# A graph network's first norm by groups of blocks, early loads of x, node numbers in PSUM, and fewer early scatters

## The reference

```python
edge_index = jnp.stack([src, dst])
h = jnp.maximum(_layernorm(x, axis=-1), 0.0)
x = x + _L0_gnn_ref(h, edge_index, L0_gnn_weight, L0_gnn_bias)
h = jnp.maximum(_layernorm(x, axis=-1), 0.0)
x = x + _L1_gnn_ref(h, edge_index, L1_gnn_W, L1_gnn_att_src, L1_gnn_att_dst, L1_gnn_bias)
...
```

```python
def mobius_add(x, y, c):
    x2 = jnp.sum(x * x, axis=-1, keepdims=True)
    y2 = jnp.sum(y * y, axis=-1, keepdims=True)
    xy = jnp.sum(x * y, axis=-1, keepdims=True)
    num = (1.0 + 2.0 * c * xy + c * y2) * x + (1.0 - c * x2) * y
    den = 1.0 + 2.0 * c * xy + c * c * x2 * y2
    return num / jnp.maximum(den, MIN_NORM)
...
def mobius_matvec(m, x, c):
    sc = jnp.sqrt(c)
    xn = _safe_norm(x)
    mx = x @ m.T
    mxn = _safe_norm(mx)
    res = jnp.tanh(mxn / xn * _artanh(sc * xn)) * mx / (mxn * sc)
...
res = proj(mobius_matvec(weight, x, c), c)
hyp_bias = proj(expmap0(b, c), c)
res = proj(mobius_add(res, hyp_bias, c), c)
xt = logmap0(res, c)
support_t = jax.ops.segment_sum(xt[s], r, num_segments=N_NODES)
```

## Time and profile before

| | us |
|---|---|
| median of 3 runs | 8386.53 (8385.81 to 8389.94) |
| the profiled execution, its own time | 8386.38 |
| its span in the profile | 8384.7 |
| POOL busy | 5866.1 (70% of the span) |
| DVE busy | 3407.2 (41%) |
| PE busy | 3380.2 (40%) |
| ACT busy | 1148.5 (14%) |

### The profile page before, as it was taken

How to read it: one execution, slowest core, us unless ns; L and a number is a source line. 1 busy time by engine, 2 the same in 40 slices (tenths; PEclk the granted TensorE clock), 3 DMA queues, 4 the chain that set the end, 5 groups by cost and what they waited for, 6 DMA issues and landing times.

```text
span 8384.7 us, 80823 instructions
## 1 busy us (share of the span) xinstructions
PE 3380.2 (40%) x13790; PEld 2554.1 (30%) x13791; DVE 3407.2 (41%) x7346; ACT 1148.5 (14%) x1948; POOL 5866.1 (70%) x5837
## 2 busy tenths in 40 slices
PE   1344443100002665442555543333345544455553
PEld 1244332100002555111444431111134444344442
DVE  4434656300004556992323323333343333433335
ACT  1000001333331111772000000000010000100001
POOL 0577777777777751787777777777757777477774
PEclk7555555555555666565555555555555555555555
DMA  1112111355553332001222222222222121111111
GB/s 39 52 51 50 45 46 33 92 135 135 135 135 84 87 86 67 19 27 39 70 70 70 69 65 77 77 76 77 76 54 52 52 53 52 48 52 53 52 52 47
DMA packets 348608, 555.47 MB, mean 66 GB/s; under 512 B 121171, under 2 KB 200871, under 8 KB 348511
## 3 DMA queue, kind: packets, MB, share of 16 engines
q0 software_dynamic: 199680, 357.35, 17.7%
q1 hardware_dynamic: 148831, 197.20, 7.8%
HBM read 448.57 MB, written 105.56 MB: 66 GB/s over the span
## 4 chain that ended last, share of the span: by engine, by line
POOL 41%; issue 21%; PE 16%; DVE 10%; DMA 7%; DVEq 4%; ACT 1%; SPq 0%; ACTq 0%; POOLq 0%
POOL GATHERED L619 34%; PE PS L730 15%; POOL list_dram L632 7%; DVE OH L1315 2%; DMA GATHERED<-row_tab,SRCI 2%; DMA GATHERED<-typed_b_tab,PLACE 2%; DVEq L317 1%; DVE OH L1309 1%; DMA GATHERED<-gat_tab,SRCI 1%; DVE T L1120 1%; DVE SM L1130 1%; DMA gat_rows<-GATHERED 1%; DMA GATHERED<-typed_tab,KEYF 1%; DVEq L319 1%; DVE T L1705 1%
## 5 line engine op out<-in xcount | busy, mean ns | idle before, releaser
L730 PE MATMUL PS<-GATHERED,OH 128*128 128x128 f32 (+2 forms) x9216 | 2434.1, 441 | 3059.1 <-DVE OH L1309 688.3
L619 POOL DMA_INDIRECT GATHERED<-row_tab,SRCI x2496 | 2466.4, 988 | 1157.8 <-issue 688.1
L730 PEld LDWEIGHTS PS<-GATHERED,OH 128*128 128x128 f32 (+1 forms) x9216 | 1899.7, 300 | 3651.7 <-issue 2182.7
L632 POOL DMA_INDIRECT list_dram<-REC,PLACE x832 | 973.8, 1170 | 507.7 <-issue 261.5
L619 POOL DMA_INDIRECT GATHERED<-typed_b_tab,PLACE x832 | 816.0, 981 | 261.7 <-issue 224.8
L619 POOL DMA_INDIRECT GATHERED<-typed_tab,KEYF x832 | 818.1, 983 | 253.6 <-issue 241.1
L619 POOL DMA_INDIRECT GATHERED<-gat_tab,SRCI x832 | 785.0, 943 | 253.6 <-issue 222.8
L1315 DVE TENSOR_SCALAR OH<-IOTA,DSTF,WF 128x128 f32 x2048 | 581.5, 360 | 433.3 <-issue 406.9
L1332 DVE TENSOR_TENSOR T<-T,PS 128x128 f32 x512 | 146.8, 287 | 962.7 <-PE PS L730 961.2
L730 PE MATMUL PS<-T,OH 128*128 128x132 f32 x2048 | 426.6, 382 | 241.2 <-DVE OH L1309 141.1
L730 PEld LDWEIGHTS PS<-T,OH 128*128 128x128 f32 x2048 | 383.1, 280 | 284.7 <-issue 193.2
(11 more groups left out here) (268 smaller groups left out, 3415.0 us busy)
## 6 DMA issues: line engine op xcount, KB each, us to landing
gat_rows<-GATHERED SPq DMA_DIRECT2D x208, 264.0 KB, 2.3
GATHERED<-gat_rows SPq DMA_DIRECT2D x208, 264.0 KB
GATHERED<-row_tab,SRCI POOLq DMA_INDIRECT x2496, 2.5
ROWI<-dst_rows SPq DMA_DIRECT2D x208, 128.0 KB
typed_b_tab<-ACC SPq DMA_DIRECT2D x49, 384.0 KB, 2.4
list_dram<-REC,PLACE POOLq DMA_INDIRECT x832
GATHERED<-gat_tab,SRCI POOLq DMA_INDIRECT x832
GATHERED<-typed_tab,KEYF POOLq DMA_INDIRECT x832, 2.5
```

Source lines behind the costliest of these rows:

```text
L619: pool.indirect_dma_start(out=rows_at[:, u * CT + t, 0:width], out_offset=None, in_=table, in_offset=bass.IndirectOffsetOnAxis(ap=rows[:, ...
L632: pool.indirect_dma_start(out=list_dram, out_offset=bass.IndirectOffsetOnAxis(ap=PLACE[:, t:t + 1], axis=0), in_=REC[:, 2 * t:2 * t + 2], ...
L730: last = mm(bank(p)[:, 0:r.shape[1]], onehot(p, t, 1, onehots_), r, start=(t == 0), stop=(t == CT - 1))
```

## The change

1. **Loads.** The weight of layer 0 and its bias come first (s_first), then x in two parts, 21 and 28 blocks (s_x), then the edges (s_edges), then everything else (s_in).
2. **First norm and product by groups.** `norm_groups("l0")` waits for parts of x alone; `dense_groups("l0")` multiplies by W0X, 129 columns, whose last is W0 times the bias, so that the product of each row with the bias falls out as a column. ACT also squares the transposed rows (HTSQ), and PE sums them with a column of ones: the row norms (HN2). `product_rows` on ACT copies the product to T, its square to H, the bias column to SM; `squared`, five groups late, sums the squares on DVE. The norm of the Moebius sum is worked out from the sums (seven operations on 128x49) and no longer from the table. The bias step goes by groups: ACT makes scaled bias rows for 49 blocks, DVE multiplies and adds, and each group has a store of its own; POOL waits for all seven.
3. **Placement.** `edge_rows`, `chunk_ends`, `edge_columns` and `source_blocks` hold what DVE did with the edges, and stand between the parts of the above, while ACT answers. Copies of WT and WL2 go from DVE to ACT, the clear of ACC from DVE to POOL.
4. **Scatters.** EARLY is 64 instead of 96; MIDDLE stays 432, so 368 follow g1.
5. **PSUM.** COLUMN (the node numbers that one-hots compare with), SAME and PLACEF (two operands of the ranks) lie in PSUM banks 2 to 7, which no walk but gb uses. COLUMN is copied again after gb's part in PSUM is over, and before l2b.

```diff
-    EARLY = 6 * BATCH
-    MIDDLE = EARLY + 21 * BATCH
+    EARLY = 4 * BATCH
+    MIDDLE = EARLY + 23 * BATCH
...
-        SAME, BEFORE, PLACEF, BUCKET = (EX[:, k * NT:(k + 1) * NT] for k in range(4))
+        BLOCK_OF, BEFORE, BUCKET = (EX[:, k * NT:(k + 1) * NT] for k in range(3))
+        PLACEF, COLUMN, SAME = (PS[:, 1024 * k:1024 * k + NT] for k in (1, 2, 3))
...
+            load(W0N, w0, s_first)
+            bcast(YROW, b0.rearrange("a b -> (a b)"), s_first)
+            for k, b0_ in enumerate(X_PARTS):
+                a, b = b0_ * GB, (X_PARTS[k + 1] * GB if k + 1 < len(X_PARTS) else NB - 1)
+                load(X3[:, a:b, :], x[a * P:b * P, :].rearrange("(b p) f -> p b f", p=P), s_x[k])
+            load(X3[0:LASTN, NB - 1, :], x[(NB - 1) * P:N, :], s_x[1])
...
+            for g in range(NG):
+                sp.wait_ge(s_tab, g + 1)
+                sp.dma_start(row_tabs[0][g * GB * P:(g + 1) * GB * P, :].rearrange("(b p) f -> p b f", p=P),
+                             group(T3, g)).then_inc(s_stored, 16)
...
+            pool.wait_ge(s_pair, 1)
+            pool.wait_ge(s_wt, 3)
+            pool.memset(ACC[:, :], 0.0).then_inc(s_zero, 1)
...
-            pool.wait_ge(s_stored, 16)
+            pool.wait_ge(s_stored, 16 * NG)
             walk("l0", row_tabs[0], D, SRCI)
...
                     for t in range(GB):
                         last = mm(product(g, t, F), HT[:, t * P:(t + 1) * P], w, start=True, stop=True)
+                    if squares:
+                        pe.wait_ge(ht_squared, n + 1)
+                        for t in range(GB):
+                            last = mm(HN2[:, g * GB + t:g * GB + t + 1], HTSQ[:, t * P:(t + 1) * P], ONE[:, :],
+                                      start=True, stop=True)
...
+            def product_rows(g):
+
+                columns_out(g, D + 1, 0, D, T3, ACT.Copy)
+                columns_out(g, D + 1, 0, D, H3, ACT.Square)
+                return columns_out(g, D + 1, D, D + 1, small(20).rearrange("p (b o) -> p b o", o=1), ACT.Copy)
...
-            norm_relu()
...
+            norm_groups("l0", X3, arrivals=X_PARTS, squares=5)
+
+            post()
+            edge_rows()
+            answered()
+            dve.sem_inc(s_rows, 1)
+            post()
+            ts(small(2), small(2), MIN_NORM, None, ALU.max)
+            chunk_ends()
+            answered()
...
-            tt(T3, T3, spread(small(21)), ALU.mult)
-            tt(H3, over(YROW, NB), spread(small(22)), ALU.mult)
-            tt(T3, T3, H3, ALU.add)
-            ask()
-            total(small(5), H3)
-            ask()
+            tt(small(5), small(5), small(21), ALU.mult)
+            tt(small(9), dot, small(22), ALU.mult)
+            stt(small(5), small(9), 2.0, small(5), ALU.mult, ALU.add)
+            tt(small(5), small(5), small(21), ALU.mult)
+            tt(small(9), small(22), small(22), ALU.mult)
+            stt(small(5), small(9), y2, small(5), ALU.mult, ALU.add)
+            ts(small(5), small(5), 0.0, None, ALU.max)
...
+            for g in range(NG):
+                tt(group(T3, g), group(T3, g), spread(group_of(21, g)), ALU.mult)
+                dve.wait_ge(n_biased, g + 1)
+                tt(group(T3, g), group(T3, g), group(H3, g), ALU.add)
+                dve.sem_inc(s_tab, 1)
...
-                                           column[:, bass.ds(c * CT, CT)].rearrange("p (t o) -> p t o", o=1)
+                                           COLUMN[:, bass.ds(c * CT, CT)].rearrange("p (t o) -> p t o", o=1)
```

More of the change, by code:

```diff
@@ L299, in program @@
         typed_mm = sem("typed_mm")
-        denses = {"l0": 0}
-        norms = {n: k for k, n in enumerate(("l1", "l2", "l3a", "l3b", "out"))}
+        norms = {n: k for k, n in enumerate(("l0", "l1", "l2", "l3a", "l3b", "out"))}
         stores = {"l3a": 1, "l3b": 2}
@@ L901, in answer, with norm_groups @@
                 nc.scalar.activation(out_, in_, fn, **kw).then_inc(s_act, 1)
[L903 to L921 removed]
+            def norm_groups(name, out_rows=None, scaled=False, relu=False, squares=False):
                 k = norms[name]
@@ L964, in attention_rows @@
-                return last
+                columns_out(g, F, 0, XW, A3, ACT.Copy)
+                return columns_out(g, F, XW, F, AM[:, :].rearrange("p (b k) -> p b k", k=HEADS), ACT.Copy)
             def scaled_rows(g):
@@ L971, in scaled_rows @@
                 return last
-            for req in requests["before_l0"]:
+            for req in requests["bias"]:
                 answer(*req)
-            dense(dn, denses["l0"], 1)
-            for req in requests["l0"]:
+            norm_groups("l0", product_rows, squares=True)
+            for req in requests["norms"]:
                 answer(*req)
+            act.wait_ge(s_wt, 2)
+            nc.scalar.activation(WT, PS[:, 0:4 * NT4 * D], ACT.Copy)
+            nc.scalar.activation(BCOL, PS[:, 2560:2560 + 2 * NT4], ACT.Copy).then_inc(s_wc, 1)
+            for req in requests["sum"]:
+                answer(*req)
+            act.wait_ge(s_wt, 3)
+            nc.scalar.activation(WL2[:, 0:NT4 * D], PS[:, 0:NT4 * D], ACT.Copy)
+            nc.scalar.activation(WL2[:, (NT4 + 1) * D:], PS[:, NT4 * D:2 * NT4 * D], ACT.Copy)
+            nc.scalar.activation(WL2[:, NT4 * D:(NT4 + 1) * D], PS[:, 2048:2048 + D], ACT.Copy).then_inc(s_wc, 1)
+            for req in requests["log"]:
+                answer(*req)
+            act.wait_ge(s_h, 2)
+            for g in range(NG):
+                for b in range(g * GB, (g + 1) * GB):
+                    last = nc.scalar.activation(H3[:, b, :], YROW, ACT.Copy, scale=small(22)[:, b:b + 1])
+                last.then_inc(n_biased, 1)
             wk = walks["l0"]
@@ new lines, in source_blocks @@
+            def source_blocks():
+                step(v.tensor_copy(SRCI[:, :], SRCF[:, :]))
+                dve.sem_inc(walks["l0"].free, RING)
+                step(v.tensor_copy(BLOCK_OF.bitcast(I32), SRCF[:, :]))
+                step(v.tensor_single_scalar(BEFORE.bitcast(I32), BLOCK_OF.bitcast(I32), 7, ALU.logical_shift_right))
+                step(v.tensor_copy(BUCKET, BEFORE.bitcast(I32)))
+                dve.wait_ge(s_drow, 64)
+                chunk_table(RANGEF, RANGES)
+                dve.sem_inc(s_info, 1)
@@ L1266, in normed, with squared @@
                     dve.sem_inc(n_normed, 1)
-                for s in range(NG + 2):
-                    for part, g in ((center, s), (variance, s - 1), (normed, s - 2)):
-                        if 0 <= g < NG:
-                            part(g)
+                def squared(g):
+                    dve.wait_ge(n_out, k * NG + g + 1)
+                    total(small(squares)[:, g * GB:(g + 1) * GB], group(H3, g))
+                parts = [(center, 0), (variance, 1), (normed, 2)] + ([(squared, 5)] if squares else [])
+                for s in range(NG + parts[-1][1]):
+                    for part, late in parts:
+                        if 0 <= s - late < NG:
+                            part(s - late)
             def artanh(o, n):
@@ L1289, in artanh, with onehots @@
                 tt(o, small(10), ser, ALU.add)
[L1291 to L1306 removed]
+            def onehots(c, b, p, weights=None, of=OH):
                 if weights is None:
@@ L1322, in all_added, with aggregate @@
                 hold(dve, wk.more_added, before + more + 1)
-            def aggregate(name, result, F, weights=None, ahead=None, column=DSTF, table=RANGES,
+            def aggregate(name, result, F, weights=None, ahead=None, table=RANGES,
                           parts=((NIT - 1, None, None),), sets=2, joins=False):
@@ L1380, in aggregate @@
                     read(0, 0, table)
[L1381 removed]
+                onehots(0, block_values(0)[2], 0, weights, of).then_inc(wk.onehot, 1)
                 start = 0
```

425 lines of the change are left out of this document (182 added, 243 removed).

## The result

The changed kernel takes 8134.89 us (median of 4 runs, 8128.51 to 8146.72), the kernel before 8388.24 us in the same series: a ratio of 0.9699, 95% interval 0.9685 to 0.9713. The forecast was 8074 us with a range of 8045 to 8130. The direction came as forecast, and so did the freeing of POOL's gathers. The size did not: the median lies 5 us above the range and 61 above the forecast, because waits between engines were left out or taken too short. The profiled execution took 8131.74 us with a span of 8130.0, 254.7 us less than before.

What follows compares the result with a forecast made beforehand. POOL and the issue time between its instructions were taken as the bound. Savings of 133 (first gather), 91 (l0 walk), 32 (scatters), 29 (l2) and 27 us (l2b) sum to 312, giving 8074 us, range 8045 to 8130.

Steps and rivals of the forecast that it cites:

- (b): What lengthens POOL's gathers: DVE operations with two SBUF inputs; PSUM operands give back 101 of the l0 walk's 106 us.
- I allow 0.4 us an iteration, 10 us in 26: l0 walk's second half: allowance for DVE being nearly the bound, making the walk's saving 91 us instead of 101.
- My own chain: DVE's operations in an iteration of the l0 walk's second half, laid out from durations: 20.0 to 20.9 us against POOL's 19.98.
- DVE becomes the bound: Rival for the l0 walk's second half: operations touching PSUM cost a little more, 23 us more, 8097 us; chance 0.08.
- It could cost up to 5.5 us; I take 0: Prelude: ACC's clear moves from DVE to POOL; cost up to 5.5 us across DVE's passes, taken as 0.
- I allow 7 us for the first groups ... Together 60: Prelude, first norm with product by groups: 60 us together, 7 of it for slow-clock first groups, ending at 71 us.
- The rival at 8095: Rival: TensorE at 1.2 GHz through the whole first norm, 9.6 us a group against 6.6, 21 us more; chance 0.07.
- g1 starts 118.5: Scatters after the l0 walk, 64 instead of 96: g1 starts 118.5 instead of 150.0 us after it, saving 32 us.
- l2: l2 walk: one-hots reading PSUM no longer delay gathers, 29 us saved; bound 0 if one-hots still block.
- l2b: l2b walk: one-hots give back 28 us, less a copy of node numbers of about 1 us, 27 us saved.
- gb: gb stage after g1: its one-hots read PSUM at no cost, change 0; growth of its 721 us would refute the forecast.
- The rest of the prelude's sum: Prelude after the first norm: conversions and scalars 41 us, bias step to 129 us limited by ACT, last store 4 us.

Runs made afterwards that it cites:

- e13: Changed kernel with the node numbers that one-hots compare with back in SBUF, on a chip with a clean g1 walk: 8220.01 us, one run.
- e14: Changed kernel with the ranks' operands SAME and PLACEF back in SBUF, on a chip with a clean g1 walk: 8158.07 us, one run.
- e5: Changed kernel with the rank in halves: comparison and scan behind the even chunk, multiply and add behind the odd: 8095.40 us, ratio to before 0.9650.
- e4: Changed kernel with the clear of ACC back on DVE behind the last bias group, on a slow chip: 9868.22 us, one run.
- e7: Changed kernel with POOL's clear of ACC waiting until DVE begins the two-input bias passes: 8133.57 us, one run.
- e8: Changed kernel without TensorE's sums of squared rows in the first norm, row norms set to constant 1: 8111.48 us, one run.
- e9: Changed kernel with rank in halves, ACC's clear beside two-input passes, and ACT replacing TensorE for row norms, on a slow chip: 9968.17 us, ratio to before 0.9987.
- e6: Changed kernel with 96 early scatters instead of 64, and 336 behind g1: 8146.02 us, one run.
- e1: Changed kernel with the node numbers that one-hots compare with back in SBUF, on a slow chip: 9765.6 us.
- e2: Changed kernel with the ranks' operands SAME and PLACEF back in SBUF, on a slow chip: 9861.15 us.

## Why the prediction was wrong

*The mechanism of (b)*, that PSUM operands free POOL's gathers, was right: -102 us of busy gathers in l0 against 101 forecast, e13 and e14 give 31 and 66 us of them back, and l3a and l3b did not move. Its wording was too narrow, and one share too small. The comparison with the bucket number (L1488) has one tensor input, in SBUF, and an SBUF output, and 14 us of the 106 lie behind it, not 9: at 498.43 us in the trace of before a gather takes 1.19 us and ends 0.1 us after one, and the only other operation beside it, an addition from PSUM, had ended 1 us earlier. It stopped holding gathers up when its output went to PSUM.

*The step that failed most* is "I allow 0.4 us an iteration, 10 us in 26". My own chain said 20.0 to 20.9 us, and the walk took 21.46: 1.5 us an iteration over the clean pace, 36 us instead of 10. The chain was put together from durations. What it missed is that with all four rank operations (5.1 us together) behind the even chunk, PE has no one-hot for that long, and that afterwards the products of two chunks, 2 us each, are due at once and DVE waits for them. e5 shows it by moving two operations and leaving everything else: the 36 us vanish. The comparison was mis-sized too (1.09 us instead of 1.02), but e5 keeps it at 1.09, so that wasn't it. The rival "DVE becomes the bound" had the place right and the cause wrong: operations that read PSUM don't cost more (scan 1946 ns against 1951, one-hots 683 against 689); only the comparison, which writes there, does.

*"It could cost up to 5.5 us; I take 0"* failed by its whole upper end. The clear did run while POOL had nothing else, but it stood beside a conversion, which ended with the clear (e4, e7). The rule of the Trainium skill (page "SBUF — State Buffer", section "SBUF: two separate sides") was the better guide there: the trace agrees with it for the conversion. The same section lets an operation with two SBUF inputs contend only with a GpSimd operation that reads SBUF, and a clear only writes; e7 agrees with that too, since the passes with two inputs keep their 1.09 us beside it. So the neighbour is what counts, and the prediction's fear for "DVE's passes" named the wrong one.

*"I allow 7 us for the first groups ... Together 60"* was 5.7 us too little, and in other executions of the same norm up to 12 (ends at up to 82.9 instead of 71). I took DVE's 6.6 us a group for the bound and the slow clock for a thing of the first groups. It was the chain TensorE and ACT, 6.75 us a group with the product alone at 1.2 GHz, to the end, and 8.8 where all was slow. The rival at 8095 ("TensorE stays at 1.2 GHz") had this mechanism. Its price of 21 us is over a norm without any slow group, so the recorded 8095 counts the 7 us of my allowance twice and should be 8088. It was an upper end, since 5.7 on top of my 7 is 12.7 and the slowest execution reaches 19. e8 and e9 show the cause: with the sums of squares gone from TensorE, the norm ends at 62.8 and 65.8.

*Scatters:* the step "g1 starts 118.5" held its form (the store of gat_tab is the next thing late, and e6 gives 24 us back) but was 8 us short. 5 us of it are DVE's own lateness at the end of the l0 walk, the square of ACC starting 12.5 us behind POOL's last gather instead of 7.3 before. The other 3 lie in the norm of l1, whose stores came slower by that much; a slow group there is the likely reason, and no run tests it. In e5, where DVE isn't late, g1 starts at 120.0.

*l2* gained 24 and not 29 us, and the reading was wrong, not the mechanism: of its gathers' 33 us of excess before, gone through one by one, only 25 lay behind one-hots and 7.5 behind typed_b's additions with two inputs in SBUF (L1811), which the change leaves alone. After it 8.4 us still lie behind them (L1818). *l2b* came out as forecast. *gb* and the rest of that stage, +5.6 us, stay open: they lie inside the spread of 712 to 735 us that nine executions show.

*The rest of the prelude's sum* held: scalars and conversions 41.9 us without the held-up one, against 41; the bias step 17.5 against 17 (though by DVE's two passes of 1.09 us a group, not by ACT); the last store 3.3 against 4.

The misses all pointed the same way: 12 + 26 + 8 + 5 + 7 us, less 1 for the rest, 57 in all. Most came from waits between two engines where the sum had only durations. One small slip of the prediction's changes nothing: 13 operations × 0.065 us × 26 are 22 us, not 23.

## What to carry to other kernels

Where one engine is freed of a delay, look at once at the pair that comes next, and lay out when each of the two has its input. Two engines that are both half idle can bound a walk, and moving half of the side work one chunk on added no operation and was worth 36 us here. A clear moved to an idle engine is free only beside operations that it doesn't hold up, so choose its neighbours. When a stage is costed by groups, take the longest chain between engines of a group, at the clock that the nearest rows show to the end and not to the second group.

## What the runs showed of the hardware

- On two chips all walks were 14 to 28% longer, and neither the change with the rank in halves (1.0011) nor the best version (0.9987) was measurably faster than the kernel before, although their first gathers came at 147 and 129 us, and the kernel before has it at 266 in its profile. The traces show where the time of the walks goes. The engines' operations keep their length there (ACT's 721 ns in g1, in the changed kernel and in e1), but the register and branch instructions between them, which don't count as busy, do not. In g1 those of ACT take 104 us in the changed kernel and 366 in e1, those of DVE 118 and 296, those of SP 44 and 263; TensorE's keep their 121 and 120. One kind of ACT's, from the two traces (count, then shortest, median and longest in ns):

```profile
L54 ACTq ALU_OP  x511: 35/35/35, 1353.0 to 2376.8; - x171
L54 ACTq ALU_OP  x505: 3/35/1397, 1549.8 to 2808.1; - x169
```

  What lengthens them on these two chips stays open, and so does why variants of the change gain so little there (e1, one run, 1.2%; e2 and e4, one run each, 0.3 and 0.2%).
